# The first cross attention of a two-layer Perceiver kernel: its two passes as two stages, or as one stage with the second pass six heads behind the first

## The reference, cut to what matters

```python
qk = jnp.einsum('bhqd,bhkd->bhqk', Q, K)
scores = qk / math.sqrt(dk)
mean_sim = scores.mean(axis=(-2, -1))
max_sim = scores.max(axis=-1).mean(axis=-1)
probs = jax.nn.softmax(scores, axis=-1)
entropy_proxy = jnp.var(probs, axis=-1, ddof=1).mean(axis=-1)
feats = jnp.stack([mean_sim, max_sim, entropy_proxy], axis=-1)
hidden = jax.nn.gelu(_linear(feats, w1, b1), approximate=False)
hidden = jax.nn.gelu(_linear(hidden, w2, b2), approximate=False)
log_t = jnp.clip(_linear(hidden, w3, b3), LOG_T_MIN, LOG_T_MAX)
t = jnp.exp(log_t)[..., None]
attn = jax.nn.softmax(qk / (2.0 * t), axis=-1)
out = jnp.einsum('bhqk,bhkd->bhqd', attn, V)
```

## Time and profile before

| | |
|---|---|
| median of 3 runs | 1384.77 us (1379.67 to 1386.34) |
| the profiled execution | 1379.86 us, span 1378.1 us |
| busy over the span | PE 1121.5, DVE 821.5, ACT 895.6, POOL 630.7 us |
| granted PE clock, mean | 0.935 |
| first pass (first to last exponential) | 54.9 to 297.6 us |
| between the passes | 297.6 to 319.4 us |
| second pass, exponentials | 319.4 to 476.0 us |

### The profile page before, as it was taken

How to read it: one execution, slowest core, us unless ns; L and a number is a source line. 1 busy time by engine, 2 the same in 40 slices (tenths; PEclk the granted TensorE clock), 3 DMA queues, 4 the chain that set the end, 5 groups by cost and what they waited for, 6 DMA issues and landing times. The chain is left out here.

```text
span 1378.1 us, 25688 instructions
## 1 busy us (share of the span) xinstructions
PE 1121.5 (81%) x8423; PEld 688.5 (50%) x8423; DVE 821.5 (60%) x1508; ACT 895.6 (65%) x1208; POOL 630.7 (46%) x293
## 2 busy tenths in 40 slices
PE   7677877857999859979987788888888888857798
PEld 3334443433444436668872444454454544434687
DVE  6788888871010175552235788888878788925312
ACT  3699999977989724533322788888888888625110
POOL 2277778760000005000002899999999999900000
PEclk9999999987999978989995899999999999968899
DMA  7874545537555061014457999999999999524140
GB/s 250 258 219 117 130 112 133 128 92 151 111 110 107 0 223 50 1 39 152 152 214 245 325 324 316 320 321 334 315 320 324 328 331 313 179 64 175 47 137 8
DMA packets 97048, 257.51 MB, mean 187 GB/s; under 512 B 11193, under 2 KB 41305, under 8 KB 85466
## 3 DMA queue, kind: packets, MB, share of 16 engines
q1 hardware_dynamic: 96992, 256.79, 59.5%
HBM read 165.31 MB, written 91.92 MB: 187 GB/s over the span
## 5 line engine op out<-in xcount | busy, mean ns | idle before, releaser
L1920 POOL TENSOR_TENSOR xb_row<-xb_row,w_mask 128x1024 f32<-128x1024 f32 x128 | 419.2, 3288 | 240.7 <-DVE xb_row L1950 239.1
L1950 DVE TENSOR_TENSOR xb_row<-xb_cont_ps,xb_row 128x1024 f32<-128x1024 f32 x128 | 156.7, 1224 | 81.0 <-PE xb_cont_ps L1750 71.9
L1750 PE MATMUL xb_rel_ps<-xb_kk,xb_qq 32*128 32x512 f32 x496 | 146.9, 670 | 35.2 <-ACT xb_out L1868 33.7
L554 DVE TENSOR_REDUCE xa_stats<-xa_b_ps 128x1 f32<-128x1024 f32 x128 | 155.6, 1219 | 33.3 <-PE xa_b_ps L470 32.6
L1961 DVE CUSTOM_DVE_ANT_0 xb_row<-xb_row,xb_minus 128x1024 f32<-128x1024 f32 x128 | 171.6, 1341 | 0.0
L1873 ACT ACTIVATE xb_row<-xb_row,xb_ntop 128x2048 f32<-128x2048 f32 x64 | 128.3, 2005 | 51.8 <-DVE xb_ntop L1967 51.8
L1750 PE MATMUL xb_cont_ps<-xb_kk,xb_qq 32*128 32x512 f32 x528 | 157.1, 672 | 2.8 <-DVE xb_row L1950 1.7
L864 ACT ACTIVATE xa_probs<-xa_psT,xa_t_now 128x1024 f32<-128x1024 f32 x128 | 141.2, 1114 | 20.3 <-PE xa_psT L823 20.1
L522 ACT ACTIVATE xa_exps<-xa_b_ps,xa_stats 128x1024 f32<-128x1024 f32 x128 | 141.2, 1108 | 12.7 <-DVE xa_stats L554 12.5
L1868 ACT COPY xb_out<-xb_rel_ps 128x1024 f32<-128x1024 f32 x124 | 124.7, 1006 | 38.0 <-PE xb_rel_ps L1750 26.6
L1787 PE MATMUL xb_turn_ps<-_ident,xb_row 128*128 128x128 f32 x1024 | 140.6, 281 | 8.3 <-ACT xb_turned L1879 7.4
(11 more groups left out here) (364 smaller groups left out, 1821.0 us busy)
## 6 DMA issues: line engine op xcount, KB each, us to landing
xb_row<-rel_scores SPq DMA_DIRECT2D x128, 512.0 KB, 6.3
rel_scores<-xb_out SPq DMA_DIRECT2D x32, 1024.5 KB, 5.6
rel_scores<-xb_out SPq DMA_DIRECT2D x32, 1024.0 KB, 5.5
b_e_w<-in_L_ffn_e_w SPq DMA_DIRECT2D x32, 513.0 KB, 3.5
w_w<-in_L_ffn_w SPq DMA_DIRECT2D x24, 512.0 KB, 4.9
xa_k<-first_parts SPq DMA_DIRECT2D x24, 384.0 KB, 5.1
value_rows<-xa_values SPq DMA_DIRECT2D x16, 544.0 KB, 6.1
xb_kk<-key_blocks SPq DMA_DIRECT2D x17, 512.0 KB, 8.1
```

Of the source, the lines that this page charges most:

```text
L554: nc.vector.tensor_reduce(stats[:, c % 2, 0, u:u + 1], ps[:, slot % 4], AX, ALU.min).then_inc(s["min_ready"], 1)
L1750: mm = nc.tensor.matmul(out[:, k * BANK:(k + 1) * BANK], qq[rows, b, kind, t * P:(t + 1) * P], kk[rows, b, half], start=True, stop=True)
L1920: nc.gpsimd.tensor_tensor(row[:, held(c), at:at + SUB], row[:, held(c), at:at + SUB], mask[:, t, half * HALF + at:half * HALF + at + SUB], ...
L1950: nc.vector.tensor_tensor(row[:, held(c), at:at + SUB], cont_ps[:], row[:, held(c), at:at + SUB], ALU.add).then_inc(s["cont_out"], 1)
```

## The change

Blocks b, c and d become one block of 22 **steps**, written out without loops. In step s the first pass works on head s (s < 16) and the second pass on head p = s - 6 (`LAG`). In each of the 8 units of a step every engine does the first pass's unit and then the second pass's group. The PSUM is divided anew: one ring of three 128x1024 tiles (`take_slot`) which scores of both passes and the net's small results take in program order; one bank `bank` for the products and for the gather of the second pass in turn (`take_bank`); one bank `sums`. The gather comes at unit 4, between products 1 and 2. From head 6 on, POOL squares five units and ACT three. The exponentials of the second pass have two SBUF tiles instead of four, keys and values of the second pass two heads instead of four. The temperature net runs for four heads at a time: maxima and weights in steps 4, 8, 12, 16, gelus in the step after, the scale one step later. `Chain` steps, all DMAs and all arithmetic of a head are as before; heads 6 to 15 have their squares divided differently.

```diff
+        LAG = 6
+        ALONE, SHARED = ((0, 2, 3, 5, 6), (1, 4, 7)), ((2, 4, 6), (0, 1, 3, 5, 7))
+        SLOTS = 3
+        GROUP = 4
+        STEPS = H + LAG
+        ring, bank_use = {}, {}
+        for step in range(STEPS):
+            p = second(step)
+            for u in range(NU):
+                if step < H:
+                    ring["first", step, u] = len(ring)
+                if u % 2 == 1 and step < H:
+                    bank_use["product", step, u // 2] = len(bank_use)
+                if u == 4 and 0 <= step - LAG - 1 < H:
+                    bank_use["both", step - LAG - 1] = len(bank_use)
+                if p is not None:
+                    ring["second", p, u] = len(ring)
...
+            ps = f.ps(inner, "b_ps", [P, SLOTS, QUARTER])
+            bank = f.ps(inner, "bank", [P, BANK])
+            sums = f.ps(inner, "sums", [P, BANK])
...
             @block.tensor
+                def take_bank(*use):
+                    if bank_use[use] > 0:
+                        pe.wait_ge(s["bank_out"], bank_use[use])
...
-                with pe.Fori(0, NB) as it:
-                    for c in range(HPB):
-                        pe.wait_ge(k_loaded[c % 2], PARTS_IN * (it * HPB // 2 + c // 2 + 1))
-                        for j in range(NU // 2):
-                            scores(it, c, 2 * j)
-                            scores(it, c, 2 * j + 1)
-                            product(it, c, j)
+                for step in range(STEPS):
+                    p = second(step)
...
+                    for u in range(NU):
+                        if u == 4 and group_at(step, 1) is not None:
+                            hidden2(group_at(step, 1))
+                        if step < H:
+                            scores(step, u)
+                        if p is not None and u >= 2:
+                            weigh(p, u - 2)
+                        elif p is not None and p > 0:
+                            weigh(p - 1, NG + u - 2)
+                        if u % 2 == 1 and step < H:
+                            product(step, u // 2)
+                        if u == 4 and 0 <= step - LAG - 1 < H:
+                            bring_together(step - LAG - 1)
+                        if p is not None:
+                            scores2(p, u)
+                        if u == 5 and group_at(step, 0) is not None:
+                            maxima(group_at(step, 0))
+                        if u == 2 and group_at(step, 1) is not None:
+                            hidden1(group_at(step, 1))
...
             @block.scalar
+                for step in range(STEPS):
+                    for u in range(NU):
+                        if step < H:
+                            exponential(step, u)
+                        if p is not None:
+                            probabilities(p, u)
+                        if u == 2 and group_at(step, 1) is not None:
+                            hidden1(group_at(step, 1))
...
+                            hidden2(group_at(step, 1))
...
+                        elif (step, u - 1) in act_index:
+                            square(step, u - 1)
...
             @block.vector
+                for step in range(STEPS):
+                    before = step - LAG - 1
+                    for u in range(NU):
+                        if step < H:
+                            minimum(step, u)
+                        if u == 0 and 1 <= step <= H:
+                            product_out(step - 1, NU // 2 - 1)
+                        if u % 2 == 0 and u > 0 and step < H:
+                            product_out(step, u // 2 - 1)
+                        if u == 1 and 0 <= before < H:
+                            take_sums(before)
+                        if u == 5 and 0 <= before < H:
+                            normalize(before)
+                        if u == 3 and 1 <= step <= H:
+                            unfold(step - 1)
+                            keep(step - 1)
...
             @block.sync
+                def load_second(p):
+                    b = p % 2
+                    if p >= 2:
+                        sp.wait_ge(s["probs_used"], NG * (p - 1))
+                    load_first_keys(f, sp, keys2[0:ROWS, b], p, kb_loaded[b])
```

788 lines of the change are left out of this document (383 added, 405 removed).

## The result

The changed kernel takes 1429.92 us (median of 4 runs, 1424.91 to 1435.92), the kernel before 1385.13 (4 runs, 1379.67 to 1386.34). The ratio is 1.034, with a 95% interval of 1.031 to 1.037: 45 us slower, where the prediction said 1389 and no more than 1411.

What follows compares the result with a forecast made beforehand. It took ACT to bound the first pass, PE and ACT the second. The terms 107 + 242 + 61 + 16 = 426 us replace 421.1, +5 us, giving 1389 us; range 1362 to 1411.

Steps and rivals of the forecast that it cites:

- (b): Six steps of the first pass alone: the one bank's closed chain, 4.47 us a pair, 17.9 a step, 107 us.
- (c): Ten steps with both passes: the bank's longer chain with the gather sets 24.2 us a step, 242 us.
- (d): Six steps of the second pass alone: key and value loads set 10.1 us a step, 61 us.
- (e): Temperature net in four groups, and the constants: partly covered, 16 us in sum, bounds 2 and 38.
- this mechanism as a rival: PE's clock falls in the first six steps: 9 us a step, two of six, 1407 us; chance 0.09.
- a clock above 0.95: Sign of the prediction's own case: granted clock above 0.95 throughout.
- its own case: The prediction's main case, the sum of its terms: 1378 to 1398 us; chance 0.36.
- (a): 20 squares move from ACT to POOL: five take POOL 20.5 us a step, costing nothing while a step is longer.
- ACT sets the shared steps: Steps with both passes: PE's bank waits lie beside ACT's work, 21.3 us a step, 1360 us; chance 0.28.
- The hand-over is dearer: Bank: 74 hand-overs on the chain, at 0.25 us more each 18 us more, 1407 us; chance 0.24.
- A change of tables empties ACT: ACT's eight table loads: nothing starts until the last exponential is out, 9 us, 1398 us; chance 0.03.
- The second pass does not run beside the first: Steps with both passes: maxima or keys late, each 14.5 + 9.8 us, the same 24.3; counted within the own case.

Runs made afterwards that it cites:

- PE kept busy: Matmuls of no effect on PE before its three kinds of wait at the bank, against the changed kernel: 1406.11 us, ratio 1.017 to the kernel before.
- the early drain: Against the changed kernel, products drained behind minimum 2j+1, one minimum earlier, and the second pass normalized behind minimum 4, not 5: 1385.79 us, ratio 1.003.
- the two-group kernel: Early drain, temperature net eight heads at a time in two groups, second pass ten steps behind, against early drain with four groups: 1370.47 us, ratio 0.991.
- the net on POOL: Two groups with early drain, but POOL does a group's subtraction (one instead of four) and its two products: 1364.04 us, ratio 0.986.

## Why the prediction was wrong

The sum was 426 us from the first to the last exponential, and the stage takes 465.9: 40 over. By its terms (a step is taken from ACT's first exponential in it to that of the next):

| term of the sum | said | measured |
|---|---|---|
| (b) six plain steps of the first pass | 107 | 106.2 |
| the start, over a plain step | nothing | 7.0 |
| (c) ten plain shared steps | 242 | 248.3 |
| (d) six plain steps of the second pass | 61 | 60.1 |
| (e) constants | 2.5 | 4.6 |
| (e) four groups of the temperature net | 13.5 | 38.3 |

The 1.4 us that are left lie between the rows. So the steps that failed are the price of the temperature net, the start, which stood at nothing, and the clock in (c).

**The bank's chain (b) was right.** Summed 4.47 us a pair and 17.9 a step; measured 4.40 and 17.7. Without it a step is 14.15.

**The start was left out.** The prediction named it among the 10.7 us that the first pass takes over its sixteen heads, and left it out of its six steps. It had the row in which DVE's first drain waits, but took from it the hand-over alone; with one bank PE stands 5.68 us behind that drain.

**The shared step (c): the waits were right, the clock was left out.** The gather and product 2 wait much as forecast (1.42 us in all nine steps, and 1.0 to 1.3 in seven, for about 1.6 each), and with PE kept busy a plain step takes 23.4 us for the 23.6 of the chain. In the change it takes 25.3: the product behind the two stands runs at half clock. The prediction had this mechanism as a rival, but for two of the first six steps only, and it named a clock above 0.95 as a sign of its own case; it was 0.87. The rival looked for PE's low share of busy time, and so to the first steps alone. There the clock fell too (0.90), behind waits of 5.68 and 4.04 us in the first step and at the constants, while products that had waited 1.54 us took their 2.05. PE is busy 86% of the shared stretch, and its clock falls there all the same. What PE did before each fall is to stand at the bank twice, 1.4 us and mostly 1.0 to 1.3. I had taken the row with a wait of 2.24 us and half clock behind it for the effect of a long wait. The ten steps exceed the sum by 6 us only, since the first of them has no gather yet and takes 20.4; against the run with PE kept busy each of the others loses 2 us.

**The temperature net (e) is the largest wrong term.** Summed 16 us with the constants, bound 38; measured 43. The groups take 6.9 + 9.3 + 12.8 + 9.3 = 38 us in the change, and with the early drain 14.1 + 15.8 + 14.3 + 7.2 = 51. Three parts of this are known. The price of a small operation, 0.22 us, came from a stretch in which POOL was nearly idle (3.87 of 21.8 us); DVE's 24 operations of a group were summed at 5.3 us and take 8.5, 8.9 and 8.8 beside POOL and 4.7 in the last group, where POOL rests. Single subtractions, products and scalings took up to 1.9 us, and the long ones that I read ended with POOL's operation. They stand between two minima on DVE, so ACT and then PE stand behind them. With ACT's slack I had covered most of it; but what was late was a minimum, in front of everything. Second, the table loads cost 8 us in all, 7 of them in the last group, for which the sum had 4 with everything; that group's steps hold the wait of 2.25 us for vhead too. Third, in the two-group kernel with the early drain, which is not the change, giving this work to POOL took 6 us off a group of 15. The rest of a group's cost is not explained: with three squares on POOL DVE's operations were nearly as short as summed, and the groups as dear. That four groups cost more than the one of 21.8 us before fits the two-group kernel: the cost goes mainly by instructions.

**The squares (a), the last steps (d).** POOL's five squares cost nothing by their time, as summed (giving them back: 2 us more, inside the interval). The last steps are at 10.04 for 10.1, but not for the reason given: the vhead load was to set their pace, and PE waited for it 2.25 us in the first of them (460.62 us) and 0.24 in one of the others (498.04). That this term came out is in part luck.

**The rivals.** *ACT sets the shared steps* (21.3 us a step) did not come in the change; it is what the early drain gives: 21.6. It was right on ACT and wrong only on how far DVE's order lets PE follow. *The hand-over is dearer* is refuted: the chain's link was 0.07 us shorter than summed. *A change of tables empties ACT*: the eight loads stand 0.02 us behind ACT's work and the next activation 0.01 behind them, so ACT is not emptied, though the loads and gelus cost nearly the 9 us of that rival by being exposed in the last group. *The second pass does not run beside the first* fails: every shared step holds both. The sentence in (c) that the overlap buys nothing at this length was right and even mild: a plain shared step is 25.3 us for the 24.3 of two heads apart in the kernel before. With the change's own drain, apart, the same heads take 17.7 + 10.0.

**Behind the stage.** The rest of the difference between the two profiled spans (50.8 us, 43.1 of them up to the last gather) is most likely the chance of two single executions: what follows the last gather takes 900.8 us in the kernel before, 908.5 in the change and 902.6 to 908.7 in the profiles of the others, and the medians are 44.8 apart.

Not settled: the rest of a group's cost, and what the first group still costs with the net on POOL, 7.3 us over a plain step in its first step. ACT waits 1.96 and 2.32 us for minima there and a product runs at half clock, but no run divides it.

## What to carry to other kernels

When a producer shares one buffer with a drain, put the drain directly behind the work that the producer needs anyway, not one unit later: here that order alone was 44 us, with the same single bank. Price small operations from rows in which the neighbouring engines do what they will do after the change, above all DVE's two-input operations beside POOL. And when PE's stands are summed, add what the clock takes behind them, even where PE is busy most of the time.

## What the runs showed of the hardware

- Two stands of PE, 1.4 us and in seven steps of nine only 1.0 to 1.3, with a gather, two sets of scores and a weighing between them, were followed by a product at the lower clock (3.48 to 3.79 us for 2.05) in nine steps of nine. Matmuls of no effect in the waits at the bank, and nothing else, brought it back to 2.05 in the plain steps and gave 24 us by the medians, 13 in the one execution that was profiled.
- A DVE product of two SBUF tiles of 128x32 elements took 0.28 us where POOL was busy 73% of the time and 0.72 where it was busy 80%; a sum over the same tile took 0.18 us in both. The 19 long products of 64 (0.40 to 1.91 us) each ended 0.05 us behind an operation of POOL.
- ACT's table loads took 1.28 us each, with 0.02 us before and 0.01 behind them. The two loads of a group cost 2 us on average, and 5 to 7 in the last group, where the first pass no longer covered them.
